# Graph kernel with two attention/GCN layers: the statistics of x, the loads of xb and x, and four low-part subtractions take other places

## The reference, cut to what matters

```python
# x: (64, 256, 512), adj: (64, 256, 256)
h = relu(layernorm(x))
q, k, v = h @ Wq.T + bq, h @ Wk.T + bk, h @ Wv.T + bv
weight = adj * exp(q @ k.T)
x = x + (weight / weight.sum(axis=2)) @ v          # layer 0
h = relu(layernorm(x))
A = adj + I;  d = A.sum(-1) ** -0.5
x = x + (A * d[:, None] * d[None, :]) @ (h @ W + b)  # layer 1
```

## Time and profile before

| | us |
|---|---|
| median of 3 runs | 1716.59 |
| lowest, highest | 1712.29, 1718.35 |
| profiled execution, its own time | 1706.24 |
| span of that execution in the trace | 1704.4 |

### The profile page before, as it was taken

How to read it: one execution, slowest core, us unless ns; L and a number is a source line. 1 busy time by engine, 2 the same in 40 slices (tenths; PEclk the granted TensorE clock), 3 DMA queues, 4 the chain that set the end, 5 groups by cost and what they waited for, 6 DMA issues and landing times.

```text
span 1704.4 us, 37784 instructions
## 1 busy us (share of the span) xinstructions
PE 1640.7 (96%) x12010; PEld 1551.3 (91%) x12010; DVE 1475.4 (87%) x3366; ACT 1060.4 (62%) x2451; POOL 831.3 (49%) x968
## 2 busy tenths in 40 slices
PE   8899999999999999999999999999999999999997
PEld 6798999999999999999998989999999999999996
DVE  5788888888888889888898889898888898888885
ACT  5656666666666666666666666666666666566552
POOL 2445445545545545545454554554554554454551
PEclk9899999999999999999999999999999999999998
DMA  5354554544544544544544544544544544545530
GB/s 171 83 146 116 124 136 118 131 132 114 139 130 118 137 126 122 137 123 121 142 122 112 148 117 117 149 120 116 151 117 117 149 120 116 146 117 122 145 100 28
DMA packets 494415, 212.66 MB, mean 125 GB/s; under 512 B 402496, under 2 KB 427072, under 8 KB 494400
## 3 DMA queue, kind: packets, MB, share of 16 engines
q1 hardware_dynamic: 492480, 210.89, 47.2%
q10 hardware_dynamic: 1920, 1.58, 0.3%
HBM read 146.28 MB, written 66.13 MB: 125 GB/s over the span
## 4 chain that ended last, share of the span: by engine, by line
DMA 28%; DVE 24%; issue 16%; SPq 14%; ACT 11%; PE 5%; POOL 1%; DVEq 0%; ACTq 0%; POOLq 0%
DMA x_in<-in_x_dram 15%; DMA h_scratch<-h 12%; SPq L185 10%; ACT unused_x L424 5%; ACT unused_x L431 5%; DVE z_lo L773 4%; DVE late L824 3%; DVE ht_lo L804 3%; DVE unused_a L793 3%; DVE p L784 3%; DVE p_lo L692 2%; DVE neg_mean L648 2%; SPq L223 2%; PE ps L836 2%; DVE v_lo L638 1%
## 5 line engine op out<-in xcount | busy, mean ns | idle before, releaser
L836 PE MATMUL ps<-ht_hi,m_hi 128*128 128x256 f32 x1024 | 287.2, 280 | 0.6 <-DVE m_lo L558 0.6
L838 PE MATMUL ps<-ht_lo,m_hi 128*128 128x256 f32 x1024 | 286.8, 280 | 0.0
L839 PE MATMUL ps<-ht_hi,m_lo 128*128 128x256 f32 x1024 | 286.4, 280 | 0.0
L408 ACT ACTIVATE g_hi<-ps,u_col 128x256 fp32r<-128x256 f32 x256 | 105.8, 464 | 251.8 <-PE ps L839 251.8
L284 POOL TENSOR_TENSOR ht_sum<-ht 128x256 f32<-128x256 f32 x64 | 47.4, 741 | 422.8 <-DVE ht L666 401.5
L836 PE MATMUL ps<-w_hi,z_hi 128*128 128x512 f32 x512 | 206.7, 404 | 38.1 <-DVE z_lo L773 38.1
L839 PE MATMUL ps<-w_hi,z_lo 128*128 128x512 f32 x512 | 202.0, 395 | 0.0
L838 PE MATMUL ps<-w_lo,z_hi 128*128 128x512 f32 x512 | 202.0, 394 | 0.0
L836 PEld LDWEIGHTS ps<-ht_hi,m_hi 128*128 128x128 f32 x1024 | 193.5, 189 | 0.7 <-DVE m_lo L558 0.7
L839 PEld LDWEIGHTS ps<-ht_hi,m_lo 128*128 128x128 f32 x1024 | 193.4, 189 | 0.0
L838 PEld LDWEIGHTS ps<-ht_lo,m_hi 128*128 128x128 f32 x1024 | 193.3, 189 | 0.0
(11 more groups left out here) (147 smaller groups left out, 5843.3 us busy)
## 6 DMA issues: line engine op xcount, KB each, us to landing
x_in<-in_x_dram SPq DMA_DIRECT2D x64, 512.0 KB, 4.3
xb<-in_x_dram SPq DMA_DIRECT2D x64, 512.0 KB, 4.9
out_dram<-late SPq DMA_DIRECT2D x128, 256.0 KB, 2.1
h_scratch<-h SPq DMA_DIRECT2D x62, 512.0 KB, 3.5
h_blocks<-h_scratch SPq DMA_DIRECT2D x248, 128.0 KB, 3.6
adj_in<-in_adj_dram SPq DMA_DIRECT2D x64, 256.0 KB, 2.9
adj_blocks<-in_adj_dram SPq DMA_DIRECT2D x256, 64.0 KB, 2.4
dn_row<-dn_scratch SPq DMA_DIRECT2D x64, 128.0 KB, 2.9
```

The source lines that it names most:

```text
L408: last = act.activation(g_hi[:, m, :], ps[:, G + j, m % 2 * N:m % 2 * N + N], ACT.Identity, bias=u_col[:, m:m + 1])
L836: pe.matmul(dst, a_hi[:, c, cols], b_hi[:, c, :], start=(first and c == 0), stop=False, skip_group_check=not first)
L838: pe.matmul(dst, a_hi[:, c, cols], b_lo[:, c, :], start=False, stop=False, skip_group_check=not first)
L839: end = pe.matmul(dst, a_lo[:, c, cols], b_hi[:, c, :], start=False, stop=(c == chunks - 1), skip_group_check=not first)
```

## The change

- The loads of `xb` and `x_in` change places on SP: `xb` is issued first.
- ACT: `x_sums` of graph `this + 2` moves from ahead of the high parts of the values to between the two exponentials, `x_squares` to behind the second one, ahead of `p_hi`. `ht_sum_hi` moves from between the exponentials to behind `ht_hi`. The row sums of adj (`keep_adjacency`) move from the end of a step to the next step, behind h.
- DVE: `neg_mean` moves to between the two halves of `p`, `ve_x` to behind the row sums, `nb_x` to behind `p_lo`. `ht_sum_lo` is now computed by DVE, behind `ht_lo` and ahead of y, and no longer by POOL behind `hat_lo`.
- POOL: `xb + bv` now stands ahead of the four sums `ht_sum`, and `rs_x` behind them.
- Steps 0 and 1 (the first two graphs): the statistics of graph 2 are taken in step 1 and not 0, those of graph 3 at the end of step 1; `w_hi` is made in step 0; the row sums of the first adjacency right behind the first h; the products of the values wait for each block of the weights apart; `ht_lo` is taken from PSUM.

Core of the diff (the part of the start-up that only moves lines is cut):

```diff
@@ sync
-                if second:
-                    x_second = x_flat[bass.ds(sp.snap((this + 1) * (N * D)), N * D)]
-                    if not prev:
-                        sp.wait_ge(h_ready[0], this + 1)
-                        sp.wait_ge(h_ready[1], this + 1)
-                    sp.dma_start(x_in[:], x_second.rearrange("(t p d) -> p t d", p=P, d=D)).then_inc(x_loaded, 16)
                 if main and prev:
                     x_this = x_flat[bass.ds(sp.snap((this - 1) * (N * D)), N * D)]
                     sp.wait_ge(x1_ready[0], this - 1)
                     sp.wait_ge(x1_ready[1], this - 1)
                     sp.dma_start(xb[:], x_this.rearrange("(t p d) -> p t d", p=P, d=D)).then_inc(xb_loaded, 16)
+                if second and prev:
+                    load_x(this)
...
@@ gpsimd
-                    if main:
-                        ht_sums_low(this)
...
-                if main and ahead and prev:
-                    pool.wait_ge(v_done[V3], this)
-                    ht_sums(this + 1)
-                if second:
-                    pool.wait_ge(ve_x_done, this + 2)
-                    pool.tensor_tensor(rs_x[:], ve_x[:], minus_half[:], ALU.pow).then_inc(rs_x_done, 1)
                 if main:
...
                         last = pool.tensor_tensor(xb[:, t, :], xb[:, t, :], bv_row[:], ALU.add)
                     last.then_inc(xb_ready, 1)
-                if main and ahead and not prev:
+                if main and not prev:
+                    x_power(this + 1)
+                if main and ahead:
                     pool.wait_ge(v_done[V3], this)
                     ht_sums(this + 1)
+                if second and main:
+                    x_power(this + 2)
@@ scalar
+            def keep_adjacency(graph, main=False):
+                act.wait_ge(adj_loaded, graph * 16)
+                if main:
+                    act.wait_ge(sd_ready, graph - 1)
...
-                if main and ahead:
+                if main and ahead and prev:
                     layer_norm_x(this, prev, older)
+                if main and prev:
+                    keep_adjacency(this, True)
...
-                    if second:
-                        x_sums(this + 2)
+                    if not prev:
+                        x_sums(this + 1)
...
-                    if second:
-                        x_squares(this + 2)
+                    if not prev:
+                        x_squares(this + 1)
...
-                    x_sums(this + 2)
-                    x_squares(this + 2)
+                    w_high()
...
                     for t in range(NT):
-                        if ahead and prev and t:
-                            ht_sums_high(this + 1)
+                        if t and not prev:
+                            layer_norm_x(this, prev, older)
+                        if t and second and prev:
+                            x_sums(this + 2)
                         act.wait_ge(s_done[t], this)
                         act.wait_ge(vk_ready[t], this)
                         act.activation(e[:, t, :], ps[:, G + t, 0:N], ACT.Exp,
                                        bias=vk[:, t:t + 1]).then_inc(e_ready[t], 1)
+                    if second and prev:
+                        x_squares(this + 2)
...
@@ vector
+            def ht_sums_low(this):
+                dve.wait_ge(ht_sum_ready, 4 * this)
+                for k in range(2):
+                    pair = slice(2 * k, 2 * k + 2)
+                    dve.wait_ge(ht_sum_hi_ready, 2 * this - 1 + k)
+                    dve.tensor_tensor(ht_sum_lo[:, pair], ht_sum[:, pair], ht_sum_hi[:, pair].bitcast(fp32),
+                                      ALU.subtract).then_inc(ht_sum_lo_ready, 1)
...
                     for t in range(NT):
+                        if t and second and prev:
+                            x_mean(this + 2)
                         dve.wait_ge(e_ready[t], this)
                         dve.tensor_tensor(p[:, t, :], e[:, t, :], adjt[:, t, :], ALU.mult).then_inc(p_ready[t], 1)
...
                 if main and prev:
+                    if second:
+                        x_variance(this + 2)
                     p_low(this)
+                    if second:
+                        x_shift(this + 2)
...
+                    if main:
+                        ht_sums_low(this + 1)
                     if not main:
...
                     elif not prev:
                         w_low()
+                        x_mean(this + 2)
+                        x_variance(this + 2)
+                        x_shift(this + 2)
```

More of the change, by code:

```diff
@@ L217, in _, with load_x @@
             adj_flat, x_flat = adj.rearrange("g n m -> (g n m)"), x.rearrange("g n d -> (g n d)")
+            def load_x(this):
+                x_second = x_flat[bass.ds(sp.snap((this + 1) * (N * D)), N * D)]
+                sp.dma_start(x_in[:], x_second.rearrange("(t p d) -> p t d", p=P, d=D)).then_inc(x_loaded, 16)
             def step(this, prev, main, ahead, older=True, second=True):
@@ L259, in step @@
                     load_blocks(sp, adj_next)
+                if second and not prev:
+                    sp.wait_ge(h_ready[0], this + 1)
+                    sp.wait_ge(h_ready[1], this + 1)
+                    load_x(this)
                 if prev:
@@ L277, in _, with x_power @@
             pool.wait_ge(ident_ready, 1)
+            def x_power(graph):
+                pool.wait_ge(ve_x_done, graph)
+                pool.tensor_tensor(rs_x[:], ve_x[:], minus_half[:], ALU.pow).then_inc(rs_x_done, 1)
             def ht_sums(this):
@@ L433, in x_squares @@
                 last.then_inc(x_square_ready, 1)
+            def keep_adjacency(graph, main=False):
+                act.wait_ge(adj_loaded, graph * 16)
+                if main:
+                    act.wait_ge(sd_ready, graph - 1)
+                for t in range(NT):
+                    last = act.activation(adj_kept[:, t, :], adj_in[:, t, :], ACT.Copy,
+                                          accum_out=rsum[:, t:t + 1])
+                last.then_inc(rsum_ready, 1)
             def hat_high(this):
@@ L473, in step @@
                     layer_norm_x(this, prev, older)
+                    keep_adjacency(this + 1)
                     for j in range(2):
@@ L514, in step @@
                                        ACT.Copy).then_inc(ht_hi_ready[j], 1)
-                    if not prev:
-                        ht_sums_high(this + 1)
-                if ahead:
-                    act.wait_ge(adj_loaded, (this + 1) * 16)
-                    if main:
-                        act.wait_ge(sd_ready, this)
-                    for t in range(NT):
-                        last = act.activation(adj_kept[:, t, :], adj_in[:, t, :], ACT.Copy,
-                                              accum_out=rsum[:, t:t + 1])
-                    last.then_inc(rsum_ready, 1)
+                    ht_sums_high(this + 1)
                 if main and not prev:
-                    w_high()
+                    x_sums(this + 2)
+                    x_squares(this + 2)
             steps(act, step)
@@ L576, in half @@
                     return wt[:, block, :, 0:HD]
+                dve.wait_ge(wvt_kept[0], 2)
+                dve.tensor_tensor(half(T1), half(T3), half(B11), ALU.subtract).then_inc(t_ready, 1)
+                bias_products()
                 dve.wait_ge(wvt_kept[1], 2)
@@ L778, in step @@
                     value_low_lower(this)
-                    if second:
-                        x_shift(this + 2)
+                    if not prev:
+                        x_shift(this + 1)
                     dve.wait_ge(adjt_ready, this)
                     for t in range(NT):
+                        if t and second and prev:
+                            x_mean(this + 2)
                         dve.wait_ge(e_ready[t], this)
```

56 lines of the change are left out of this document (29 added, 27 removed).

## The result

| | before | changed |
|---|---|---|
| median of 4 runs | 1714.44 us | 1743.31 us |
| lowest to highest | 1708.28 to 1718.35 | 1739.33 to 1747.68 |
| ratio, 95% interval | | 1.0172 (1.0127 to 1.0217) |
| profiled execution, span | 1706.24, 1704.4 | 1746.51, 1744.7 |

The account below looks back on a forecast made before the run. The bound was a closed loop through y, SP, DMA and DVE. Terms summed to +0.64 us a turn, +38 us in 59 turns, less 4.5 at start-up; put on the 1716.6 median: 1750 us, own range 1722 to 1778.

Parts of the forecast that it names:

- What bounds the kernel: Steady turn: closed loop from y over SP and DMAs to the transposes of h, then by DVE to y; 25.69 us mean.
- x leaves the chain to z: DVE, transposes of h to y: x steps leave, -1.52 us per turn; their return further down costs +0.30.
- Squares 0.42: ACT, ahead of p_hi: squares wait for neg_mean and delay p_hi, +0.42 us per turn (0 to 0.9).
- diagonal 0.44: POOL's diagonal additions and DVE's ht_sum_lo hold each other up; one addition passes between the subtractions, +0.44 us (0 to 0.5).
- `ht_sum_lo` and diagonal together 1.64: Between ht_lo and y: two subtractions on DVE, +1.20 us per turn, plus the hold by POOL's diagonal, +0.44.
- xb ahead: -0.20: POOL: addition to xb ahead of x and the four sums, -0.2 us per turn (-0.6 to +0.4).
- T to y 14.6: T is the start of the transposes of h; from there to y's end 14.6 us instead of 13.96.
- Start-up -4.5: First graphs: g_hi comes earlier and the wait at w_lo goes, -4.5 us in all (-7 to -2).
- The stall of PE: PE's wait for z_lo ahead of O1: 38.1 us in all before, to become 80 to 100 us.
- A (1665): Rival: stall goes and PE is the bound, T to y under 13.43 us, 1665 us; chance 0.13.
- B: Rival: holds from squares, diagonal and xb do not come, turn -0.2 to -0.6 us, 1699 us; chance 0.12.
- C: Rival: steady part unchanged, xb lands and holds as x_in did, only start-up gained, 1712 us; chance 0.10.

Follow-up runs that it names:

- xb last: Changed kernel with POOL's addition to xb behind the four sums again, load of xb still first: 1754.57 us, ratio 1.0214.
- the two kernels that PE bounds: Changed kernel and kernel before, each with h_scratch ahead of adj_in and the stores of y on SP, on one chip: 1651.41 and 1653.07 us.
- no squares: Changed kernel without the squares of x in the steady steps, variance taken from an old value: 1727.0 us, ratio 1.0062.
- diagonal late: Changed kernel with POOL's additions to the diagonal held back until ht_sum_lo is done: 1730.1 us, ratio 1.0096.
- h first: SP sends h_scratch ahead of adj_in and stores of y: changed kernel 1650.74 us, that with ht_sum_lo on POOL 1652.55, kernel before 1654.82.

## Why the prediction was right, and where it was off

**What bounds the kernel: right.** That the turn is a closed loop, and not a busy engine, carries the whole forecast. It is shown from both halves: two subtractions put in between T and y cost about what they take (27.30 against 25.69), the same work behind y costs nothing that shows (25.06), and time taken out between y and T comes back until PE is the bound (24.83).

**x leaves the chain to z: right, sized together with the others.** The terms without `ht_sum_lo` and diagonal gave -1.00 us, and 0.94 was measured. The agreement is of their sum: neither the -1.52 nor the +0.30 was measured by itself. That "what `nb_x` had waited for falls on p" was right in part: a half of p takes 676 ns in the mean, and took 429, so the two halves are 0.49 us longer, while `nb_x` fell from 1215 ns to 162.

**Squares 0.42, measured 0.32 to 0.33; diagonal 0.44, measured 0.22 to 0.33; `ht_sum_lo` and diagonal together 1.64, measured 1.4 to 1.6.** Where two figures stand, one is from the two traces and the other from the medians or ratios. A whole addition was let pass between the two subtractions, and DVE is longer by 0.26 us only; no `ht_sum_lo` takes over 1 us, as had been named. What the removal of either saves includes whatever else shifts with it.

**xb ahead: -0.20, measured -0.14 (26.36 against 26.50), within the noise.** The prediction named the value sum or the upper `v_lo` at 0.8 us or more; the sum came at 1158 ns. The Trainium skill ("SBUF — State Buffer", section "Who interferes with whom") says that a VectorE instruction with both inputs in SBUF and a GpSimd instruction that reads SBUF contend, and that the lock is exclusive. By this rule `z_lo` was to gain less than the x steps free, and the traces agree: it starts 5.37 - 4.69 = 0.68 us sooner in the mean, and with xb last 5.37 - 3.97 = 1.40. What this costs ahead of `z_lo` comes back behind it: T to y is 14.55 us in the mean with xb ahead, and 14.76 with xb last.

**T to y 14.6: right.** The turn shown has 14.45, and the mean over the steady turns is 14.55. y to T was held to be untouched, and it grew by 0.10 us only (means 11.67 and 11.77); the 11.39 of the prediction was that of one quick turn. The forecast of +0.64 us a turn and the 0.67 between the traces (26.36 - 25.69) agree better than two executions of one kernel do: from the 29 us between the medians a turn has lost about 0.5 us. That much of the agreement is luck.

**Start-up -4.5: too much, and gone at graph 4.** Graph 3 starts at 84.71, and in the kernel before it was 90.14: 5.4 us sooner. But 2.5 us of that stand already at the first matmul of graph 1 (26.20 and 28.70), whose start lies anywhere from 26.2 to 30.0 in kernels with the changed start-up, so 2.9 us are the change's. Graph 4 starts at 115.13, against 115.08. Step 3 gave it all back, and the timelines of SP and DVE show one reason:

```profile
86.63 0.38 SPq L233 DMA_DIRECT2D h_scratch<-h  x1
92.86 2.89 SPq L185 DMA_DIRECT2D h_blocks<-h_scratch  x4
...
98.95 1.31 DVE L679 STREAM_TRANSPOSE ht<-h_blocks 128x512 f32<-128x512 f32 x2 [3.16 <-DMA h_blocks<-h_scratch]
```

h_scratch took 92.86 - 86.63 = 6.2 us until SP could start the blocks, where it lands in about 3.5 in a later turn. PE then waits 3.33 us for `z_lo` in this turn. This term of the sum was mis-sized: between the two kernels that PE bounds graph 4 starts 1.9 us sooner, and the medians differ by 1.7. Why the store took so long in that step is open. It is no accident of one execution: in this step the store took 5.0 to 6.0 us in the three experiments with `ht_sum_lo` ahead of y and the changed start-up (xb last, no squares, diagonal late), and 3.7 or 3.8 with `ht_sum_lo` on POOL or behind y. Between the profiled executions the forecast was a span of 1738, and 1744.7 came: 4.5 us are this term, 1.6 the turns (39.6 against 38) and 0.6 the end. Between the medians it was 1750 and 1743.31 came, because the change was put on a median 10 us above its profiled execution, and the changed kernel's lies 3 us below its own.

**The stall of PE: right in kind, too high.** 80 to 100 us were named, 67.4 came. Part of the reason is told in the last section: in 8 turns PE ran its next stage at a lower clock, 1.55 us longer, and the turn behind each had no stall for `z_lo`, or 0.3 us at most. That makes some 12 us.

**The rivals.** A (1665) would have been the kernel without `ht_sum_lo` in the loop, 1669.69: the argument against it, 1.2 us in a loop that had none to spare, is what decided. B fell because the holds came: without the squares 0.33 us a turn go, and without the meeting of `ht_sum_lo` and the diagonal 0.22 to 0.33. C fell because the turn is 0.67 us longer; xb landed where x_in had, 1.1 us behind T, as both the forecast and C said. What the prediction left unsaid is that the whole loop could be shortened on SP's side though no engine does less.

## What to carry to other kernels

When PE stands still once a turn for one small operation, follow the chain until it comes back to where it began, and test both of its halves. Here two subtractions inside the loop cost about their full length, the same two just behind its last link nothing that shows, and the squares, 1.5 us of ACT work inside it that DVE's own work hides in part, 0.33 us. Engine load tells nothing of this (DVE was busy for 87% before and after). Look at the DMA queue in the loop first: two stores of late data that no one needs soon, and a load, issued ahead of the store of h that the next turn's transposes hang on, cost this kernel 51 us, 3% of its time, and another order on the queue mends it.

## What the runs showed of the hardware

**After a long stall the next stage of PE can be slower.** PE timeline and windows of the changed kernel. The windows give us of the stretch, then busy us (x instructions) of PE, PEld, DVE, ACT and POOL, the granted clock, the DMA share and GB/s; the first is O1 of graph 4's turn, the second that of the next:

```profile
159.42 0.69 PE L862 MATMUL ps<-w_hi,z_hi 128*128 128x512 f32 x1 [2.35 <-DVE z_lo L791]
...
132.00:137.60 5.60, 5.60 (x24) 4.58 (x25) 5.17 (x16) 4.55 (x12) 1.75 (x3) 1.00 0.09 13
159.50:166.60 7.10, 7.10 (x24) 5.65 (x25) 6.67 (x18) 6.10 (x14) 3.20 (x4) 0.76 0.04 6
```

From the start of the first to the end of the last, the same 24 matmuls take 7.38 us in the second turn and 5.82 in the first (the windows leave out the last tenths). The granted clock of the second is 0.76 in the mean, so part of it ran at the level of 1.2 GHz and the rest at 2.4. This was so in 8 turns of the changed kernel and 25 of the one with `ht_sum_lo` on DVE alone (its stalls are longer, 93.5 / 59 = 1.6 us in the mean, and its clock is 0.968 over the span), in 2 or 3 turns of those with xb last, without the squares and with the diagonal late, and in none of the kernel before and of those with `ht_sum_lo` on POOL, behind y, or with h first, whose longest waits for `z_lo` are 1.5 or 1.6 us. The slower stages came after stalls of 1.8 to 3.3 us. Not every such stall brought one: in the changed kernel a stage after another stall of 2.35 us kept the full clock, and in the one with `ht_sum_lo` on DVE alone stages after 2.19, 2.65 and 2.69 us did.

It did not lengthen the turn. In the changed kernel the 8 turns with such a stage take 26.2 us from T to the next T in the mean, and the others 26.4: the loop through SP and DVE sets the turn, and PE's longer stage takes the place of the next turn's stall. Even so, the two executions with a granted clock of 0.987 took 1746.51 and 1747.68 us, and those with 0.993 and 0.995 took 1740.11 and 1739.33. Longer stalls would explain both the time and the clock, but this was not tested.

**DVE and POOL hold each other up one instruction at a time.** The two subtractions `ht_sum_lo` beside the two additions to the diagonal took 1.55 and 1.62 us in the steady turns of the changed kernel; with the diagonal held back they took 1.29 and 0.88, in the mean. The 0.26 us that DVE loses is less than one addition of 0.44, and far less than both. An instruction of two elements a partition pays the same way: `nb_x` took 1215 ns in the mean beside the addition to xb in the kernel before, and 162 in the changed one.
